# A four-layer attention kernel: layer 2's head-spread operand built in eight parts, and another table of steps for the stages without layer 2

## The chip, the cores and the metric

The kernel runs on one core of one Trainium2 chip. The metric is the device time of one execution in microseconds. Engines are named as in the profile: PE (TensorE), DVE (VectorE), ACT (ScalarE), POOL (GpSimd), SP (SyncE, which here only issues DMAs).

## What is computed

Four attention layers run one after the other on x (8 batches, 100 rows, 128 columns), 16 heads of 8. Layers 0, 1 and 3 attend to a context of 1444 keys; layer 2 attends to the context's first 100 rows with a causal mask, and has a feed-forward part.

```python
x = _L0_xattn_ref(x, ctx_1024, ...)    # rmsnorm(x), rmsnorm(ctx), attention, @ wo.T
x = _L1_xattn_ref(x, ctx_1024, ctx_1024, mask, ...)   # masked attention, @ Wo.T, + x, layer norm
x = _L2_xattn_ref(x, ctx_1024, ...)    # causal, so only the first 100 keys count; FF of 512, gelu
x = _L3_xattn_ref(x, ctx_1024, ctx_1024, ...)         # attention, + x, layer norm
# in each:
scores = einsum('bhqd,bhkd->bhqk', q, k) * scale
o = einsum('bhqk,bhkd->bhqd', softmax(scores), v)
```

## The kernel before

**Units, stages and steps.** The work on the long context is cut into 24 units: layer 0, 1 and 3 for each of the 8 batches. A unit's scores are made in 48 tiles, 12 chunks of about 120 keys by 4 groups of four heads (400 columns, `QW`). The whole program is a pipeline of stages n = -3 to 24, each of 48 steps j (`NSTEP`). In stage n the unit n is in its `exp` role (scores once more, exponential on ACT, product with the values into `acc`), unit n-1 is `post` (output, projection, norms), unit n+1 is `top` (values, maxima), and unit n+2 is `prep` (context, inputs, queries, keys); unit n+3 is `load`. Layer 2 has no unit of its own. Its attention (`att2`) is carried in stages 12 to 19 and its norm and feed-forward (`ff2`) in stages 13 to 20.

**What sets the order.** Every engine's order is written by hand from two tables: `AT` says at which step j of a stage the pieces of layers 0, 1 and 3 stand, `AT2` and `AT2_FF` do so for layer 2. In each step PE issues one score tile for the exponential (`sexp`, three banks), one score tile for the row maximum (`ring`), every fourth step 16 products into `acc`, and then whatever the tables put at that step. DVE takes the maximum tile into `mx` (L1251, in the first chunk L1249), then its share of the tables' pieces: `kp` (L1228 for layers 1 and 3, L1231 for layer 0) at the step after k0, k1 and k2, `qs` (L1238) at the step of q, output and norm pieces at steps counted from O (7) and wo (15), `ssq` (L1213) at 25 and 28. ACT takes the exponential at each step, and `kp`'s high part, the copies of xT, q and v at theirs. An engine works strictly in its written order, so that one that waits holds all that is behind it.

**The ring.** All of PE's products other than `sexp` and `acc` share four PSUM banks, `ring0` to `ring3`. `place` walks through all steps ahead of time and gives each use the bank that is free first by a table of holding times (`HOLD`); PE then waits, before it writes a bank, until the bank's last holder has been read (`await_read`). Keys hold their bank until DVE's `kp`, queries until DVE's `qs`.

**Layer 2's operand.** POOL turns layer 2's keys into an operand that is zero outside a head's 8 rows (`spread2`, L518): `kbd2` has two halves (high and low part, index i) of 16 heads by 100 columns. Its source is one half of `kq16`, the 16-bit copies of `k2`. PE's four score products of layer 2 (`scores2`, steps 20 to 23) wait for it. Behind `spread2` on POOL stands `root` (L506): `rstd`, the reciprocal root of the norm in `ff2`. DVE's `scale` (L1281) at step 13 waits for it. Behind `root` POOL spreads the next unit's queries into `qx` (L535) once DVE has made `qs`, and later takes the maxima off layer 2's scores (L526).

## Time and profile before

| what | value |
|---|---|
| median of 3 runs | 1046.35 us (1047.9, 1038.03, 1046.35) |
| the profiled execution | 1042.32 us; its span 1040.5 us |
| PE busy | 940.1 us, 90% |
| DVE busy | 852.9 us, 82% |
| ACT busy | 721.5 us, 69% |
| POOL busy | 376.2 us, 36% |
| mean granted TensorE clock | 0.967 of full speed |
| chain that ended last | PE 60%, DVE 26%, ACT 5%, issue 4%, POOL 3%, DMA 2% |

The profiled execution was 4.0 us below the median of the runs. Busy times are those of the records. PE's matmuls overlap: four products of 400 columns are issued in 0.17 us and the record of the group is 0.34 us long, so a gap between records of PE is about 0.17 us shorter than the gap between issues.

### The profile page before, as it was taken

What the parts mean: (1) busy time and instruction counts of PE and PEld (TensorE: products, weight loads), DVE (VectorE), ACT (ScalarE), POOL (GpSimd) and SP (SyncE); (2) the same over time, 40 slices, a digit from 0 to 9 for tenths busy, and PEclk for the clock granted to TensorE, in tenths of its full rate; (3) what the DMA queues carried; (4) which work ended last, traced back from release to release, by engine and by line L of the source; (5) the groups of instructions that cost most, each with busy time, mean ns of one, the idle gap of its engine ahead of it and who ended that gap; (6) DMA issues with size and microseconds to landing.
All of it is one profiled execution on the core that took longest, in us unless ns stands there. A gap on an engine that the chain in (4) does not pass through costs nothing.

```text
span 1040.5 us, 43899 instructions
## 1 busy us (share of the span) xinstructions
PE 940.1 (90%) x18826; PEld 554.9 (53%) x18826; DVE 852.9 (82%) x1804; ACT 721.5 (69%) x1637; POOL 376.2 (36%) x404
## 2 busy tenths in 40 slices
PE   1889999999989999999989899899989898999996
PEld 1345556555546555555555555555555555555552
DVE  7887899889778898888988787888797878779851
ACT  1129777777767777777767767677677666677776
POOL 3845445444323232322353444344352515122000
PEclk9669999999999999999999999999999898999999
DMA  8322313232222333233223131212121221222100
GB/s 227 111 63 65 93 50 89 70 78 60 79 84 61 97 99 96 60 95 96 62 85 86 37 88 52 73 35 72 37 70 49 61 56 53 56 66 62 53 4 6
DMA packets 63641, 73.75 MB, mean 71 GB/s; under 512 B 8130, under 2 KB 59114, under 8 KB 63318
## 3 DMA queue, kind: packets, MB, share of 16 engines
q1 hardware_dynamic: 63446, 70.92, 24.3%
q8 instruction: 150, 2.46, 1.0%
q14 instruction: 45, 0.37, 0.1%
HBM read 50.35 MB, written 18.15 MB: 66 GB/s over the span
## 4 chain that ended last, share of the span: by engine, by line
PE 60%; DVE 26%; ACT 5%; issue 4%; POOL 3%; DMA 2%; SPq 1%; POOLq 0%; ACTq 0%; DVEq 0%
PE ring L609 23%; PE sexp L609 13%; PE acc L779 13%; DVE mx L1251 7%; PE ring L652 5%; DVE mneg L1257 5%; DVE mx L1249 4%; POOL kbd L518 2%; PE ring L836 1%; PE ring L629 1%; ACT probs L1031 1%; DMA qx<-mrow 1%; DVE qs L1238 1%; PE ring L790 1%; DMA rows<-in_rows 1%
## 5 line engine op out<-in xcount | busy, mean ns | idle before, releaser
L1251 DVE TENSOR_TENSOR mx<-ring,mx 120x400 f16<-120x400 f32 (+1 forms) x1056 | 563.0, 564 | 111.2 <-PE ring L609 104.9
L1031 ACT ACTIVATE probs<-sexp 120x400 f32<-120x400 f32 (+1 forms) x1152 | 531.7, 508 | 174.4 <-PE sexp L609 171.9
L609 PE MATMUL ring<-qx,krep 96*32 96x400 f16 (+2 forms) x4608 | 415.0, 346 | 30.7 <-DVE mx L1249 13.3
L609 PE MATMUL sexp<-qx,krep 97*32 97x400 f16 (+2 forms) x4608 | 410.3, 339 | 11.4 <-ACT probs L1031 7.3
L779 PE MATMUL acc<-probs,vx 120*18 120x200 f32 (+1 forms) x4608 | 253.8, 337 | 0.8 <-ACT probs L1031 0.7
L609 PEld LDWEIGHTS ring<-qx,krep 96*32 96x32 f16 (+2 forms) x4608 | 129.7, 98 | 126.3 <-DVE mx L1251 36.2
L609 PEld LDWEIGHTS sexp<-qx,krep 97*32 97x32 f16 (+2 forms) x4608 | 131.5, 96 | 101.8 <-ACT probs L1031 34.6
L779 PEld LDWEIGHTS acc<-probs,vx 120*18 120x18 f32 (+1 forms) x4608 | 131.4, 99 | 66.9 <-issue 4.5
L498 POOL CAST ct<-ctf 128x480 f16<-128x480 f32 (+1 forms) x69 | 41.5, 601 | 202.7 <-PE ring L652 143.2
L535 POOL TENSOR_TENSOR qx<-qs,headmask 96x400 f16<-96x400 f16 x96 | 80.0, 862 | 73.8 <-DVE qs L1238 73.7
L500 POOL TENSOR_TENSOR ct<-ctf,ct 128x480 f16<-128x480 f32 (+1 forms) x69 | 76.4, 1107 | 5.5
L652 PEld LDWEIGHTS ring<-wv,ct 128*120 128x120 f16 (+1 forms) x864 | 54.8, 136 | 26.8 <-DVE mx L1251 11.9
L652 PE MATMUL ring<-wv,ct 128*120 128x128 f16 (+1 forms) x864 | 64.9, 226 | 2.5 <-DVE mx L1251 1.5
L1249 DVE CAST mx<-ring 121x400 f16<-121x400 f32 x96 | 52.7, 565 | 15.2 <-PE ring L609 15.1
L609 PE MATMUL ring<-ct,wk 128*32 128x480 f16 (+1 forms) x864 | 60.0, 383 | 4.1 <-DVE mx L1251 2.9
L506 POOL TENSOR_TENSOR rstd<-vare,half 100x1 f32<-100x1 f32 x24 | 13.3, 556 | 131.7 <-DVE vare L1273 131.7
L1257 DVE TENSOR_REDUCE mneg<-ring 100x8 f16<-100x968 f16 x48 | 55.3, 1154 | 1.0 <-PE ring L735 1.0
L1001 ACT COPY vx<-ring 120x512 f32<-120x512 f32 (+1 forms) x72 | 42.4, 589 | 13.2 <-PE ring L652 10.1
L991 ACT ACTIVATE kp<-ring,cols 128x480 f16<-128x480 f32 (+1 forms) x48 | 31.8, 663 | 26.2 <-PE ring L609 26.2
L518 POOL TENSOR_TENSOR kbd<-kq,heads 128x1600 f16<-128x1600 f16 x16 | 45.8, 2881 | 0.6
L513 POOL CAST kq<-k 128x200 f16<-128x200 f32 x8 | 2.8, 352 | 96.1 <-ACT v L1054 96.1
L545 POOL CAST maskb<-mask 100x480 bf16<-100x480 uint8 (+1 forms) x24 | 13.4, 597 | 62.4 <-DMA mask<-in_mask 62.4
(139 smaller groups left out, 895.6 us busy)
## 6 DMA issues: line engine op xcount, KB each, us to landing
krep<-kept SPq DMA_DIRECT2D x144, 120.0 KB, 2.8
ctf<-in_ctxT SPq DMA_DIRECT2D x16, 722.0 KB
kept<-kp SPq DMA_DIRECT2D x48, 240.0 KB, 3.1
krep<-kept SPq DMA_DIRECT2D x72, 121.0 KB, 2.6
kept<-kp SPq DMA_DIRECT2D x24, 242.0 KB, 2.8
nat<-in_ctx SPq DMA_DIRECT2D x8, 720.0 KB
maskexp<-maskmax SPq DMA_DIRECT2D x8, 281.2 KB, 3.4
anymask<-in_mask SPq DMA_DIRECT2D x1, 1128.1 KB, 10.0
```

Source lines behind the costliest of these rows:

```text
L498: pool.tensor_copy(ct[:, u.par, 0, c0:c0 + n], ctf[:, c0:c0 + n]).then_inc(sem["ct_high"], 1)
L500: pool.tensor_tensor(ct[:, u.par, 1, c0:c0 + n], ctf[:, c0:c0 + n], ct[:, u.par, 0, c0:c0 + n], ALU.subtract).then_inc(sem["ct_low"], 1)
L518: last = pool.tensor_tensor(kbd2[:, i, :, :], kq16[:, i, 0, :].unsqueeze(1).broadcast_to([128, H, S]), heads16[:, :].unsqueeze(2).broadcas ...
L535: last = pool.tensor_tensor(qx[0:PARTS, u.third, t, :, :], qs[:, t, :].unsqueeze(1).broadcast_to([PARTS, HT, S]), headmask16[:, :].unsquee ...
L609: last = run(out[g:g + m], w[:, g:g + m], x, **flags)
L652: last = pe.matmul(ps[0:r, D * i:D * i + D], ct[:, u.par, p, c0:c0 + r], wv16[:, w, u.L, :], start=(j == 0), stop=(j == 2))
L779: last = pe.matmul(acc[32 * q:32 * q + VW, 2 * S * side:2 * S * side + 2 * S], vx[0:r, u.par, PAIRS * c + 2 * t + p, :], probs[0:r, j % PR ...
L1001: act.copy(vx[0:r, u.par, a0:a1, :].rearrange("p a (f e) -> p a f e", f=2)[:, :, :, 0:DH], bank(f"v{g}", u)[0:r, 0:2 * DH * (a1 - a0)].rea ...
L1031: act.activation(probs[0:r, j % PR, :], sexp[j % SR][0:r, 0:QW], ACT.Exp).then_inc(sem["probs_ready"], 1)
L1249: op = dve.tensor_copy(dst, src)
L1251: op = dve.tensor_tensor(dst, src, dst, ALU.max)
L1257: dve.tensor_reduce(mneg[:, 8 * i:8 * i + 8], bank(f"mt{i}", u)[0:S, :].bitcast(F16).rearrange("s (h n) -> s h n", h=8)[:, :, 0:chunk(0)[1 ...
```

## The change

There are two edits. The first: POOL's two instructions of 1600 columns for `kbd2` become eight of 400, for each group t of four heads the high and the low half, and the semaphore `kbd2_ready` counts 4 per batch in place of 1. PE's `scores2` waits for part t+1 ahead of group t, where it waited once ahead of the first. The second: a new table `AT_PLAIN` holds in every stage in which neither `att2` nor `ff2` is there: stages -2 to 11 and 21 of those with a `prep` unit (stage 22 has values only). In it xT stands at step 18 (13 before), q at 20 (16), k1 at 22 (24), v0 at 24 (25), mk0 at 25 (26), v1 at 27 (28), mk1 at 28 (29), k2 at 30 (31), mk2 at 31 (32). k0 (10), OT (12), wo (15), v2 (33), the norm steps and the maxima stay. Since `place` gives out the banks from these steps, the banks of later products change as well.

```diff
+AT_PLAIN = dict(AT, xT=18, q=20, k1=22, v0=24, mk0=25, v1=27, mk1=28, k2=30, mk2=31)
...
-                          "kq2_high": 1, "kq2_low": 1, "kbd2_ready": 1, "s2_filled": 4, "s2_read": 4, "max2_ready": 4, "less2_ready": 4,
+                          "kq2_high": 1, "kq2_low": 1, "kbd2_ready": T, "s2_filled": 4, "s2_read": 4, "max2_ready": 4, "less2_ready": 4,
...
+        def steps_of(s):
+
+            return AT if s.att2 is not None or s.ff2 is not None else AT_PLAIN
...
-                for i in range(2):
-                    last = pool.tensor_tensor(kbd2[:, i, :, :], kq16[:, i, 0, :].unsqueeze(1).broadcast_to([128, H, S]),
-                                              heads16[:, :].unsqueeze(2).broadcast_to([128, H, S]), ALU.mult)
-                last.then_inc(sem["kbd2_ready"], 1)
+                for t in range(T):
+                    h = slice(HT * t, HT * t + HT)
+                    for i in range(2):
+                        last = pool.tensor_tensor(kbd2[:, i, h, :], kq16[:, i, 0, :].unsqueeze(1).broadcast_to([128, HT, S]),
+                                                  heads16[:, h].unsqueeze(2).broadcast_to([128, HT, S]), ALU.mult)
+                    last.then_inc(sem["kbd2_ready"], 1)
...
-                if t == 0:
-                    pe.wait_ge(*at("kbd2_ready", u, 1))
+                pe.wait_ge(*at("kbd2_ready", u, t + 1))
...
-                    if s.prep is not None and j == AT["q"]:
+                    if s.prep is not None and j == steps_of(s)["q"]:
                         queries(s.prep)
```

All other uses of `AT[...]` in the loops of PE, ACT and DVE and in `other_products` become `steps_of(s)[...]` in the same way.

**PE, steps 12 to 14 of stage 3.** `ident,oatt` is OT at step 12, `ident,xall` is xT, `qx,krep` into a ring bank is a maximum tile, into sexp the tile for the exponential. k0 was put into ring2 at step 10 before the change, and into ring3 after it. Before:

```order
L609 MATMUL ring3<-ident,oatt 32x100 x4
L609 MATMUL sexp1<-qx,krep 32x400 x3
L609 MATMUL sexp1<-qx,krep 25x400
L609 MATMUL ring0<-qx,krep 32x400 x4
L609 MATMUL ring2<-ident,xall 32x100 x4
L609 MATMUL sexp2<-qx,krep 32x400 x3
L609 MATMUL sexp2<-qx,krep 25x400
L609 MATMUL ring1<-qx,krep 32x400 x4
L779 MATMUL acc<-probs,vx 18x200 x8
```

Of the changed kernel, the same place:

```order
L617 MATMUL ring1<-ident,oatt 32x100 x4
L617 MATMUL sexp1<-qx,krep 32x400 x3
L617 MATMUL sexp1<-qx,krep 25x400
L617 MATMUL ring0<-qx,krep 32x400 x4
L617 MATMUL sexp2<-qx,krep 32x400 x3
L617 MATMUL sexp2<-qx,krep 25x400
L617 MATMUL ring3<-qx,krep 32x400 x4
L787 MATMUL acc<-probs,vx 18x200 x8
```

xT is gone from there, and the next to use k0's bank is the maximum tile of step 14, one `sexp` tile later.

**DVE, steps 15 to 24 of the same stage.** `y` (L1320) and `xall` (L1324) are the two pieces behind the projection, `qs` is the queries' piece, `kp` that of the keys. Before:

```order
L1251 TENSOR_TENSOR mx<-ring2,mx 120x400
L1320 TENSOR_TENSOR y<-ring0,rows 100x128
L1238 SCALAR_TENSOR_TENSOR qs<-qh,headmask,ring1 96x400
L1251 TENSOR_TENSOR mx<-ring3,mx 120x400
L1324 TENSOR_TENSOR xall<-y,xall 100x128
L1251 TENSOR_TENSOR mx<-ring0,mx 120x400
L1251 TENSOR_TENSOR mx<-ring2,mx 120x400
```

Of the changed kernel, from the same piece `y` on:

```order
L1327 TENSOR_TENSOR y<-ring1,rows 100x128
L1258 TENSOR_TENSOR mx<-ring3,mx 120x400
L1331 TENSOR_TENSOR xall<-y,xall 100x128
L1258 TENSOR_TENSOR mx<-ring2,mx 120x400
L1258 TENSOR_TENSOR mx<-ring0,mx 120x400
L1258 TENSOR_TENSOR mx<-ring3,mx 120x400
L1245 SCALAR_TENSOR_TENSOR qs<-qh,headmask,ring2 96x400
L1258 TENSOR_TENSOR mx<-ring1,mx 120x400
L1258 TENSOR_TENSOR mx<-ring0,mx 120x400
L1258 TENSOR_TENSOR mx<-ring1,mx 120x400
L1238 TENSOR_TENSOR kp<-ring3,kp 128x480
```

`qs` no longer stands between `y` and `xall` but three maximum tiles behind them, and three tiles ahead of the next keys' `kp`; before, nine stood between.

**POOL, in stage 13.** `rstd` is the root for layer 2's norm. Before:

```order
L513 CAST kq16<-k2 128x200
L515 TENSOR_TENSOR kq16<-k2,kq16 128x200
L518 TENSOR_TENSOR kbd2<-kq16,heads16 128x1600 x2
L506 TENSOR_TENSOR rstd<-vare,half 100x1
L545 CAST maskb<-mask8 100x484
```

Of the changed kernel:

```order
L519 CAST kq16<-k2 128x200
L521 TENSOR_TENSOR kq16<-k2,kq16 128x200
L526 TENSOR_TENSOR kbd2<-kq16,heads16 128x400 x8
L512 TENSOR_TENSOR rstd<-vare,half 100x1
L553 CAST maskb<-mask8 100x484
```

Nothing changes its place on POOL; `rstd` stands behind eight instructions in place of two.

## Rows read from the trace of the kernel before

**Rows 1.** Busy by stretch: us; PE, PEld, DVE, ACT, POOL (instructions); PEclk, DMA, GB/s

```profile
183.07:219.50 36.43, 35.58 (x733) 21.36 (x729) 32.14 (x65) 27.65 (x63) 16.80 (x16) 1.00 0.28 74
368.33:403.92 35.59, 34.34 (x736) 20.94 (x732) 30.46 (x61) 27.27 (x63) 9.94 (x13) 1.00 0.31 88
403.92:440.60 36.68, 34.70 (x736) 20.99 (x732) 32.60 (x69) 27.26 (x63) 10.54 (x14) 1.00 0.29 85
656.55:704.04 47.49, 43.56 (x915) 25.90 (x908) 39.47 (x92) 34.41 (x80) 19.58 (x20) 1.00 0.21 59
800.30:850.10 49.80, 44.59 (x888) 27.01 (x884) 40.80 (x90) 34.26 (x80) 19.72 (x20) 0.92 0.20 57
```

**Rows 2.** Timeline of PE, stage 3: start, us, line, out<-in, [idle before <-releaser]

```profile
197.26 0.38 PE L609 MATMUL ring<-ident,xall 100*32 100x100 f32 x8 [0.21 <-DVE kp L1231]
...
202.47 0.34 PE L609 MATMUL ring<-qx,krep 96*32 96x400 f16 x4
202.64 0.34 PE L609 MATMUL sexp<-qx,krep 97*32 97x400 f16 x4
203.26 0.35 PE L609 MATMUL ring<-qx,krep 96*32 96x400 f16 x4 [0.28 <-DVE mx L1251]
```

**Rows 3.** Timeline of PE, stage 9

```profile
416.38 0.38 PE L609 MATMUL ring<-ident,xall 100*32 100x100 f32 x8 [0.37 <-DVE kp L1228]
...
422.69 0.35 PE L609 MATMUL ring<-qx,krep 96*32 96x400 f16 x4 [0.28 <-DVE mx L1251]
...
425.32 0.79 PE L609 MATMUL ring<-ct,wk 128*32 128x480 f16 x12 [0.61 <-DVE mx L1251]
...
433.53 0.88 PE L652 MATMUL ring<-wv,ct 128*120 128x128 f16 x12 [0.25 <-DVE mx L1251]
```

**Rows 4.** Chain that ended last, stage 15: start, us, what

```profile
665.98 5.72 POOL kbd L518 x2
671.70 0.52 POOL rstd L506
```

**Rows 5.** Timelines of DVE and PE, stage 15

```profile
672.24 0.35 DVE L1281 SCALAR_TENSOR_TENSOR xn<-xn,rstd,rows 100x128 f32<-100x128 f32 x1 [1.19 <-POOL rstd L506]
```

```profile
677.42 0.70 PE L609 MATMUL ring<-kbd,kq 128*32 128x400 f16 x12
```

**Rows 6.** One line's instructions: ns min/median/max, first and last start, forms

```profile
L518 POOL TENSOR_TENSOR kbd<-kq,heads x16: 2857/2881/2906, 523.5 to 863.6; 128x1600 f16<-128x1600 f16 x16
```

```profile
L535 POOL TENSOR_TENSOR qx<-qs,headmask x96: 846/852/902, 29.3 to 961.7; 96x400 f16<-96x400 f16 x96
```

```profile
L1314 DVE TENSOR_TENSOR y<-y,xall x8: 278/292/2455, 765.5 to 1035.7; 100x128 f32<-100x128 f32 x8
```

**Rows 7.** Timeline of DVE, stage 18

```profile
811.47 0.98 DVE L1311 TENSOR_TENSOR y<-oatt,rows 100x128 f32<-100x128 f32 x1
...
812.85 2.46 DVE L1314 TENSOR_TENSOR y<-y,xall 100x128 f32<-100x128 f32 x1
...
817.21 0.34 DVE L1281 SCALAR_TENSOR_TENSOR xn<-xn,rstd,rows 100x128 f32<-100x128 f32 x1
```

**Rows 8.** Timeline of POOL, stages 17 and 18

```profile
762.09 5.72 POOL L518 TENSOR_TENSOR kbd<-kq,heads 128x1600 f16<-128x1600 f16 x2
...
776.87 0.85 POOL L526 TENSOR_TENSOR sc<-sc,max 100x400 f32<-100x400 f32 x1 [0.77 <-DVE max L1338]
```

```profile
809.44 5.72 POOL L518 TENSOR_TENSOR kbd<-kq,heads 128x1600 f16<-128x1600 f16 x2
...
826.51 0.85 POOL L526 TENSOR_TENSOR sc<-sc,max 100x400 f32<-100x400 f32 x1 [0.75 <-DVE max L1338]
```

**Rows 9.** Busy time by stretch, two microseconds each, stages 17 and 18

```profile
766.00:768.00 2.00, 0.28 (x11) 0.00 (x0) 2.00 (x2) 0.97 (x4) 2.00 (x2) 1.00 0.00 0
...
814.00:816.00 2.00, 0.00 (x2) 0.01 (x2) 2.00 (x3) 0.23 (x1) 1.72 (x2) 0.69 0.00 0
816.00:818.00 2.00, 2.00 (x28) 0.97 (x32) 2.00 (x7) 0.00 (x0) 0.00 (x0) 0.50 0.36 123
```

More of the change, by code:

```diff
@@ L271, in other_products @@
             for g in range(3):
-                if prep is not None and prep.L == 0 and j == AT[f"ct{g}"]:
+                if prep is not None and prep.L == 0 and j == steps_of(s)[f"ct{g}"]:
                     uses.append((f"ct{g}", prep))
-                if prep is not None and j == AT[f"k{g}"]:
+                if prep is not None and j == steps_of(s)[f"k{g}"]:
                     uses.append((f"k{g}", prep))
-                if prep is not None and prep.L == 1 and j == AT[f"mk{g}"]:
+                if prep is not None and prep.L == 1 and j == steps_of(s)[f"mk{g}"]:
                     uses.append((f"mk{g}", prep))
-                if top is not None and j == AT[f"v{g}"]:
+                if top is not None and j == steps_of(s)[f"v{g}"]:
                     uses.append((f"v{g}", top))
@@ L281, in other_products @@
                            ("mn", top)):
-                if u is not None and j == AT[use] and not (use in ("OT", "wo") and u.L == 3):
+                if u is not None and j == steps_of(s)[use] and not (use in ("OT", "wo") and u.L == 3):
                     uses.append((use, u))
@@ L1086, in stage @@
                     for g in range(3):
[L1087 removed]
+                        if s.prep is not None and s.prep.L == 0 and j == steps_of(s)[f"ct{g}"]:
                             context(s.prep, g, s.top)
[L1089 removed]
+                        if s.prep is not None and j == steps_of(s)[f"k{g}"]:
                             keys(s.prep, g)
[L1091 removed]
+                        if s.prep is not None and s.prep.L == 1 and j == steps_of(s)[f"mk{g}"]:
                             mask(s.prep, g)
[L1093 removed]
+                        if s.top is not None and j == steps_of(s)[f"v{g}"]:
                             vals(s.top, g)
[L1095 removed]
+                    if s.post is not None and s.post.L < 3 and j == steps_of(s)["OT"]:
                         output_back(s.post)
[L1097 removed]
+                    if s.prep is not None and j == steps_of(s)["xT"]:
                         inputs(s.prep)
[L1099 removed]
+                    if s.prep is not None and j == steps_of(s)["q"]:
                         queries(s.prep)
@@ L1106, in stage @@
                                        ).then_inc(sem["mask_counted"], 1)
-                    if s.top is not None and j == AT["mn"]:
+                    if s.top is not None and j == steps_of(s)["mn"]:
                         maximum_rows(s.top)
@@ L1416, in stage @@
                         for part in range(4):
-                            if j == AT["O"] + 1 + part:
+                            if j == steps_of(s)["O"] + 1 + part:
                                 output(u, part)
-                            if u.L == 3 and j == AT["O"] + 5 + part:
+                            if u.L == 3 and j == steps_of(s)["O"] + 5 + part:
                                 centre(u, y[:, 0, :], "own_o", part)
-                            if u.L == 1 and j == AT["wo"] + 3 + part:
+                            if u.L == 1 and j == steps_of(s)["wo"] + 3 + part:
                                 centre(u, y[:, 0, :], "own_y", part)
                         for part in range(2):
-                            if u.L < 3 and j == AT["wo"] + 1 + part:
+                            if u.L < 3 and j == steps_of(s)["wo"] + 1 + part:
                                 projected(u, part)
-                            if u.L == 1 and j == AT["scale"] + part:
+                            if u.L == 1 and j == steps_of(s)["scale"] + part:
                                 scale(u, residual(u), "x_next", part)
-                            if u.L == 3 and j == AT["scale"] + part:
+                            if u.L == 3 and j == steps_of(s)["scale"] + part:
                                 if part == 1:
@@ L1432, in stage @@
                     for g in range(3):
-                        if s.prep is not None and j == AT[f"k{g}"] + 1:
+                        if s.prep is not None and j == steps_of(s)[f"k{g}"] + 1:
                             keys(s.prep, g)
-                    if s.prep is not None and j == AT["q"]:
+                    if s.prep is not None and j == steps_of(s)["q"]:
                         queries(s.prep)
                     for part in range(2):
-                        if s.load is not None and s.load.L == 0 and j == AT["power"] + 3 * part:
+                        if s.load is not None and s.load.L == 0 and j == steps_of(s)["power"] + 3 * part:
                             power(s.load, part)
                     for i in range(2):
-                        if s.top is not None and j == AT[f"mt{i}"]:
+                        if s.top is not None and j == steps_of(s)[f"mt{i}"]:
                             maxima(s.top, i)
```

33 lines of the change are left out of this document (13 added, 20 removed).

## The prediction

> **What bounds the kernel now.** I read the busy times by stretch first. Between two copies of the maxima, that is over one stage, a stage without layer 2 takes 36.43 us (stage 3, layer 0 in preparation), 35.59 (stage 8) and 36.68 (stage 9, where a layer 1 unit is normed as well); one with layer 2 takes 47.49 (stage 15) and 49.80 (stage 18) [rows 1]. PE is busy for 35.58 of 36.43 us and 43.56 of 47.49, DVE for 32.14 and 39.47. PE sets the pace, and what can be gained is where PE waits for a bank of the ring that DVE has not read.
>
> Second, the timeline of PE. In it four products are issued 0.17 us apart from the next four though each record is 0.34 long, so an idle time shown is short of the real stall by 0.17 [rows 2]. Stage 3 then has two stalls that this change touches. xT waits for k0's bank, 0.21 + 0.17 = 0.38 us, and a maximum tile some steps behind the queries waits 0.28 + 0.17 = 0.45 [rows 2]. Stage 9 has four: 0.37 + 0.17 = 0.54 at xT, 0.45 behind the queries, 0.61 + 0.17 = 0.78 at k1, and 0.25 + 0.17 = 0.42 at v2, which stands two steps behind k2 [rows 3].
>
> Third, the chain that ended last, in the stages with layer 2. In stage 15 it runs through both `kbd` instructions (5.72 us), then `rstd` (0.52) [rows 4], then DVE's `xn`, which had waited 1.19 us for it [rows 5]. PE's first product on `kbd` starts at 677.42 [rows 5], and `kbd` was whole at 665.98 + 5.72 = 671.70 [rows 4]: nobody waits for the operand itself. What is late is the small root that stands behind it on POOL. The two microsecond slices and DVE's rows of stages 17 and 18 I come to below.
>
> **Edit 1, eight parts for two, stages 13 to 16.** An instruction of 1600 columns takes 2.881 us, one of 400 columns of the same kind takes 0.852 [rows 6]. The slope is (2.881 - 0.852) / 1200 = 1.69 ns a column, the fixed part 0.852 - 400 x 0.00169 = 0.18 us. Eight parts take 8 x 0.852 = 6.82 us where two took 5.72 [rows 4]: +1.1 us. The bounds are 8 x 2.857 / 4 = 5.71 (no fixed part, +0) and 8 x 0.902 = 7.22 (+1.5) [rows 6]. I take 6.82, since `qx` is the same operation with the same kinds of operands. `rstd` and the waiting `xn` move by as much, and the chain passes through them. So the early first part brings nothing here, and the late end costs 4 x 1.1 = +4.4 us. Stage 12 has no `ff2`, so no root behind `kbd`: 0. The three added waits of PE are met long before, 0.
>
> **Edit 1, stages 17 to 19.** Here DVE's `y` (L1314), two operands in SBUF, takes 2.455 us at most and 0.292 as a median [rows 6]. In stage 18 it runs from 812.85 to 815.31, and `kbd` from 809.44 to 815.16; the one ahead, L1311, runs from 811.47 to 812.45, and the first `kbd` ended at 809.44 + 2.86 = 812.30 [rows 7, 8]. Both end just behind an end of a POOL instruction. I read it as DVE being held until the POOL instruction that is under way is over. With parts of 0.85 us it is held for 0.85 at most, on the mean 0.43: L1314 takes about 0.7, 1.7 us less. But `xn` stands behind it and needs `rstd`, at 809.44 + 6.82 + 0.52 = 816.78, and started at 817.21 [rows 7, 8]. So of the 1.7 us only 817.21 - 816.8 = 0.4 arrive: 3 x 0.4 = -1.2 us.
>
> DVE gets its turn at the end of a POOL instruction, and hardly holds POOL back: the two `kbd` of stage 18, with L1311 falling between them, took the same 5.72 us as those of stage 15 [rows 4, 8]. So I put nothing on POOL for it. The Trainium skill (SBUF — State Buffer, section "SBUF: two separate sides") says that the port pair which VectorE and GpSimd share is a lock, held for a whole instruction, and that the loser blocks fully, whichever it is. By the first half of that rule L1314's wait shrinks as I have it; by the second each such VectorE operation between two parts adds its own length to POOL, and the sum would be that of the last rival below.
>
> **Edit 1 and the clock.** In stage 18 the stall behind L1314 leaves PE idle, and the granted clock falls from 1.00 to 0.50 (1.2 GHz of 2.4) at 814 to 816; in stage 17 PE is busy 0.28 us of two and the clock stays at 1.00 [rows 9]. The price is the time from `kbd` to the first subtraction of a maximum: 826.51 - 809.44 = 17.07 us with the fall, 776.87 - 762.09 = 14.78 without [rows 8]. That is 2.3 us. In stage 19 the clock falls at the same place. If DVE's stall is cut into pieces, as above, PE takes several tiles in between; I take it that both falls go: -4.6 us. Bounds: 0 and -4.6.
>
> **Edit 2.** Behind k0 the next user of its bank comes one `sexp` tile (0.17 us) later and no longer is xT, so that 0.38 becomes about 0.2 and 0.54 about 0.35; moved to 18, xT finds a bank read long ago. I take 0.2 us per stage. The queries, now at 20, lie clear of `y` and `xall`, and nothing of DVE's other than one norm step is at their side, so I take the 0.45 as gone. k2 a step earlier puts its `kp` two steps ahead of v2: the 0.42 goes. Of the 0.78 at k1 in stages with a norm I take half, 0.4: the norm steps stand where they did, and DVE's load in that stretch is the same. What hides the rest: `qx` is spread on POOL in four parts of 0.852 [rows 6] and is needed at step 35; even four steps later (four times 36.43 / 48 = 3.0 us) it is ready by about step 28.
>
> Sums: stages 0 to 5, (0.2 + 0.45) x 6 = 3.9. Stages 6 to 8, (0.2 + 0.45 + 0.42) x 3 = 3.2. Stages 9 to 11, (0.2 + 0.45 + 0.42 + 0.4) x 3 = 4.4. Stages -2, -1, 21: 0, the first two wait for loads and for DVE. Together -11.5. The bounds are 0 and all of the stalls, 0.83 x 6 + 1.25 x 3 + 2.19 x 3 = 15.3.
>
> **Sum.** +4.4 - 1.2 - 4.6 - 11.5 = -12.9 us. Against the profiled execution: 1042.3 - 12.9 = 1029.4. The median of the runs shown lies 4.0 above that execution, so the median would be 1033; I write 1032, a little under, since a collision of `xall` and of two norm steps with `qx` on POOL goes too, which I can't size.
>
> **Rivals.**
> - *The stalls move instead of going.* DVE's work in the stretch from step 16 to 34 is the same and it is busy 32.14 of 36.43 us [rows 1]; q, k1 and v0 now stand at 20, 22 and 24, close together. For it: PE's slack over DVE is small. Against: a stall moves only where DVE is behind by three tiles. Then edit 2 gives a third, 4 us, and the sum is -5.4: 1037 by the profile, 1040 by the median.
> - *The clock falls elsewhere.* In stages 13 to 16 the wait for `rstd` grows from 1.19 to 2.3 us, nearly the length at which stage 18 fell. Four falls cost 4 x 2.3 = 9.2, and the sum is -3.7, near 1042. For it: rows 9 show that the same idle time may or may not bring a fall. Against: PE has tiles in hand during a part of the wait.
> - *Slower: two banks held at once.* q at 20 and k1 at 22 each take a bank until ACT and then DVE have gone over them, as k0 does, where it costs 0.54 [rows 3]. If the maxima have two banks left for four steps, and each of these steps stalls by that much, that is 4 x 0.54 = 2.2 us a stage, over 12 stages 26, and the sum is +13: 1059 by the median. It turns the sum to a loss from a new stall of 12.9 / 12 = 1.1 us a stage. Against: DVE comes to these pieces with less behind it than it does now.
> - *POOL is held by DVE between parts.* Eight parts have seven places between them where two had one. If in stages 13 to 19 three two-operand pieces of DVE get in, each 0.29 long [rows 6], and POOL waits them out, `rstd` is late by 7 x 3 x 0.29 = 6 us more in all; the sum is -6.8, near 1039. Against: the unchanged 5.72 above. It is what the page's rule gives.
>
> **How the numbers follow.** Chances: forecast 0.46 (by its own bounds 1025 to 1037); stalls move 0.22; clock falls elsewhere 0.14; POOL held 0.07; slower 0.11. A measurement of this kernel tells about 1% from no change, that is 10.5 us. Of the forecast nine tenths lie over 1% faster, of the second a third (less lost than I say), of the others little: 0.41 + 0.07 + 0.03 = 0.51 faster. Slower by over 1% is the two banks' case and a little of the clock's: 0.12. The rest, 0.37, is within 1%. The range goes from 1022 (all the stalls of edit 2 gone, 3.8 more, and some of the collisions) to 1047, which leaves the slower case and part of the clock's out.
>
> **What would show it.** In the profile of the changed kernel: eight `kbd` of about 0.85 us, 6.8 in all, with `rstd` right behind; DVE's `xn` in stages 13 to 16 waiting 2.2 to 2.4 us; L1314's longest under 1.2 us; no clock of 0.50 inside stages 18 and 19; stage 3 at 35.8, stage 8 at 34.5 and stage 9 at 35.2 us; stage 15 at 48.6. I am wrong if stages 3 and 9 are as long as before, if a stall of over 0.4 us stands at k1 or v0 of every stage, if PE waits for `kbd` in `scores2`, or if the granted clock falls in stages 13 to 16.

## The result and the profile after

The changed kernel takes 1034.64 us in the median (1031.91 to 1039.88, 20 runs), the kernel before 1044.57 in the same comparison (1038.03 to 1049.48, 20 runs). The ratio is 0.9911, with a 95% interval of 0.9897 to 0.9925: 0.9% faster. That is within the 1% that I had called the limit of what can be told from no change; the interval does exclude 1. I had written 1032 us, with a range of 1022 to 1047, and "faster by over 1%" as the likeliest case.

The page of the changed kernel, its head, its rows of slices and its chain:

```profile
span 1030.1 us, 43971 instructions
...
PE 934.3 (91%) x18826; PEld 559.9 (54%) x18826; DVE 837.4 (81%) x1804; ACT 717.6 (70%) x1637; POOL 382.4 (37%) x452
...
PEclk9669999999999999999999999999999999999999
...
PE 60%; DVE 22%; POOL 6%; ACT 5%; issue 4%; DMA 2%; SPq 1%; POOLq 0%; ACTq 0%; DVEq 0%
```

The span is 10.4 us shorter (1040.5 before). PE still has the longest busy time and the largest part of the chain, so what moved are stalls and the granted clock.

The stretches of stages 3, 8, 9, 15 and 18, cut at the same copies of the maxima and in the same columns as [rows 1]:

```profile
182.85:219.24 36.39, 35.78 (x733) 21.82 (x729) 31.70 (x65) 27.29 (x62) 16.76 (x16) 1.00 0.27 74
368.18:403.32 35.14, 34.37 (x736) 21.20 (x732) 29.94 (x61) 26.94 (x62) 9.89 (x13) 1.00 0.31 89
403.32:438.65 35.33, 34.54 (x736) 21.57 (x732) 31.57 (x69) 26.93 (x62) 10.40 (x14) 1.00 0.31 88
653.98:702.24 48.26, 43.33 (x915) 25.94 (x908) 39.19 (x92) 34.42 (x81) 20.45 (x26) 1.00 0.20 58
797.16:843.96 46.80, 42.54 (x900) 25.47 (x892) 38.92 (x91) 34.05 (x80) 20.63 (x26) 1.00 0.22 61
```

Stage 3 is as long as it was, stages 8 and 9 are shorter by 0.45 and 1.35 us, stage 15 is longer by 0.77 and stage 18 shorter by 3.00. The profiled executions are not all typical of their kernels: the changed kernel's took 1031.91 us (2.7 under its median), that of the parts alone 1039.63 (0.6 under), and that of the table alone 1034.4, the fastest of its 12 (5.5 under). The whole table, as differences of stage lengths to the kernel before in one profiled execution of each (us; "parts only" and "table only" are the first two experiments below, "root ahead" is the fifth):

| stages | forecast | after | parts only | table only | root ahead, eight parts |
|---|---|---|---|---|---|
| 2, 3, 4, 5 | -0.65 each | -0.33, -0.04, +0.03, -0.49 | +0.02, -0.01, +0.01, -0.18 | -0.32, -0.12, +0.07, -0.82 | 0.00, +0.07, +0.20, -0.79 |
| 7, 8 | -1.07 each | -0.54, -0.45 | 0.00, +0.01 | -0.53, -0.43 | -0.53, -0.43 |
| 9, 10, 11 | -1.47 each | -1.35, -1.65, -1.77 | +0.01, -0.13, +0.04 | -1.51, -1.51, -1.80 | -1.54, -1.64, -1.54 |
| 13, 14, 15, 16 | +1.1 each | +1.54, +1.54, +0.77, +0.52 | +0.87, +1.31, +0.63, +2.67 | +0.01, -0.01, -0.25, -0.35 | -1.82, -0.87, -1.06, +0.11 |
| 17 | -0.4 | -1.81 | -1.81 | -1.28 | -0.86 |
| 18, 19 | -2.7 each | -3.01, -3.28 | -1.78, -3.95 | +0.02, 0.00 | -2.06, -5.17 |
| 20 | 0 | -1.46 | -0.40 | +0.11 | -1.46 |
| 21 | 0 | +0.44 | 0.00 | +0.46 | +0.44 |

Stages 0, 1 and 6 moved by -0.43, +0.88 and +1.11, where -0.65, -0.65 and -1.07 were forecast; stage -1 took -0.34, stage 12 -0.28. Stage 6 lies between -1.4 and +1.9 over the experiments, and much of that is the clock: it is shortest with the table alone, whose clock stays at 1.00 there, where that of the kernel before has a mean of 0.96. All of it adds up to -10.4 us.

The eight parts. One line's instructions (ns: minimum, median, maximum), then the timelines of POOL and DVE in stage 16:

```profile
L526 POOL TENSOR_TENSOR kbd<-kq,heads x64: 847/855/904, 518.1 to 858.9; 128x400 f16<-128x400 f16 x64
```

```profile
711.42 6.59 POOL L526 TENSOR_TENSOR kbd<-kq,heads 128x400 f16<-128x400 f16 x8
717.97 0.55 POOL L512 TENSOR_TENSOR rstd<-vare,half 100x1 f32<-100x1 f32 x1
...
718.55 0.35 DVE L1288 SCALAR_TENSOR_TENSOR xn<-xn,rstd,rows 100x128 f32<-100x128 f32 x1 [2.43 <-POOL rstd L512]
```

A part takes 0.855 us, eight of them 6.59 where two took 5.72 [rows 4]; the root stands right behind, and DVE waits 2.43 us for it, where it waited 1.19 [rows 5].

DVE and then POOL in stage 18, the place of [rows 7, 8]:

```profile
808.37 0.61 DVE L1318 TENSOR_TENSOR y<-oatt,rows 100x128 f32<-100x128 f32 x1
...
809.38 0.45 DVE L1321 TENSOR_TENSOR y<-y,xall 100x128 f32<-100x128 f32 x1
...
813.58 0.35 DVE L1288 SCALAR_TENSOR_TENSOR xn<-xn,rstd,rows 100x128 f32<-100x128 f32 x1 [1.26 <-POOL rstd L512]
```

```profile
806.35 6.68 POOL L526 TENSOR_TENSOR kbd<-kq,heads 128x400 f16<-128x400 f16 x8
...
820.57 0.85 POOL L534 TENSOR_TENSOR sc<-sc,max 100x400 f32<-100x400 f32 x1 [0.75 <-DVE max L1345]
```

`y` (L1314 before, L1321 now) takes 0.45 us where it took 2.46, the other `y` 0.61 for 0.98, and from `kbd` to the first subtraction of a maximum it is 820.57 - 806.35 = 14.22 us, for 17.07.

The clock, in two-microsecond stretches. First the kernel before at the border of stages 16 and 17 and in stage 19, then the changed kernel at the same two places:

```profile
750.00:752.00 2.00, 2.00 (x33) 1.25 (x28) 0.92 (x3) 1.15 (x4) 0.00 (x0) 0.50 0.04 8
...
868.00:870.00 2.00, 2.00 (x32) 0.93 (x24) 1.88 (x8) 0.36 (x1) 0.00 (x0) 0.50 0.39 132
```

```profile
749.00:751.00 2.00, 2.00 (x45) 1.36 (x37) 1.30 (x3) 1.40 (x4) 0.00 (x0) 1.00 0.00 0
...
864.00:866.00 2.00, 2.00 (x42) 1.63 (x38) 0.72 (x2) 0.95 (x2) 2.00 (x4) 0.51 0.00 0
```

To compare kernels I cut stages 11 to 21 into stretches of one microsecond and added up the length of each times what its clock lacked to 1.00, where that was over 0.03. By stage, in us:

| kernel | 13 | 14 | 15 | 16 | 17 | 18 | 19 | 20 | sum |
|---|---|---|---|---|---|---|---|---|---|
| before | 0 | 0 | 0 | 0.85 | 0.85 | 4.00 | 5.18 | 1.06 | 11.9 |
| after | 1.71 | 1.71 | 0 | 0 | 0 | 0 | 1.71 | 0 | 5.1 |
| parts only | 0 | 0 | 0.43 | 2.96 | 0 | 1.71 | 1.11 | 0.60 | 6.8 |
| table only | 0 | 0 | 0 | 0 | 0 | 3.88 | 5.19 | 1.17 | 10.2 |
| root ahead, eight parts | 0 | 0 | 0.42 | 1.64 | 1.69 | 1.34 | 0 | 0 | 5.1 |

About 6.8 us of clock were won in this execution. One execution is one draw, though. Span and mean granted clock are known of every execution. Span times what its mean clock lacked to 1.00 is the same sum over the whole span, start included. It is the most that the clock can have cost, since PE also waits in it. What is left of the span is in the last column (us):

| kernel | executions | clock lost, mean | the rest, mean |
|---|---|---|---|
| before (beside the two halves) | 23 | 32.6 | 1010.0 |
| after | 20 | 27.4 | 1006.0 |
| parts only | 12 | 25.4 | 1012.4 |
| table only | 12 | 34.5 | 1003.2 |

The standard errors are 0.8 to 1.6 us in the third column and 0.9 to 1.2 in the fourth. So the change wins 5.2 us of clock and 4.0 of the rest. The parts win 7.2 us of clock and lengthen the rest by 2.4. The table shortens the rest by 6.8 and wins no clock (+1.9, about its error); the execution that its stage lengths are from lost 20.7 us, 14 less than its mean.

### The profile page after: what moved, and what is told of

The parts are those of the page before. It is cut to its first block, busy times and chain, and to the rows that moved or that the text cites. A ratio compares the mean times of both kernels' runs of the same rounds, so it can differ in the third digit from the quotient of the medians.

```text
span 1030.1 us, 43971 instructions
## 1 busy us (share of the span) xinstructions
PE 934.3 (91%) x18826; PEld 559.9 (54%) x18826; DVE 837.4 (81%) x1804; ACT 717.6 (70%) x1637; POOL 382.4 (37%) x452
## 4 chain that ended last, share of the span: by engine, by line
PE 60%; DVE 22%; POOL 6%; ACT 5%; issue 4%; DMA 2%; SPq 1%; POOLq 0%; ACTq 0%; DVEq 0%
PE ring L617 23%; PE sexp L617 14%; PE acc L787 13%; DVE mx L1258 6%; PE ring L660 5%; DVE mneg L1264 5%; POOL kbd L526 5%; DVE mx L1256 4%; ACT probs L1038 2%; PE ring L843 1%; PE ring L637 1%; DMA rows<-in_rows 1%; DVE kp L1235 1%; DVE ssq L1220 1%; PE ring L798 1%
## 5 line engine op out<-in xcount | busy, mean ns | idle before, releaser
L617 PE MATMUL ring<-ct,wk 128*32 128x480 f16 (+1 forms) x864 | 63.5, 383 | 1.8 <-DVE mx L1258 0.8
L526 POOL TENSOR_TENSOR kbd<-kq,heads 128x400 f16<-128x400 f16 x64 | 53.0, 863 | 0.6
```

The costliest lines, as they stand in the source:

```text
L526: last = pool.tensor_tensor(kbd2[:, i, h, :], kq16[:, i, 0, :].unsqueeze(1).broadcast_to([128, HT, S]), heads16[:, h].unsqueeze(2).broadca ...
L617: last = run(out[g:g + m], w[:, g:g + m], x, **flags)
```

## The experiments

All were compared with the kernel before on their own chip. The theory at the start was that of the prediction: the late root costs stages 13 to 16, the shorter holds of DVE pay in 17 to 19, the new table pays in the stages without layer 2.

### The two halves apart

The parts alone:

```diff
-AT_PLAIN = dict(AT, xT=18, q=20, k1=22, v0=24, mk0=25, v1=27, mk1=28, k2=30, mk2=31)
+AT_PLAIN = AT
```

> Edit 1 alone: eight parts, the old steps in all stages. Theory (the eight parts lengthen kbd and so rstd in stages 13 to 16, and take DVE's hold of 2.4 us away in 17 to 19): stages -1 to 11 and 21 as before within 0.1 us each; stages 13 to 16 longer by 0.5 to 1.5 us each; 17 to 19 shorter by 1.8 to 3.3; in all 5 to 6 us less than before, ratio near 0.995. Rival (the gain of the change lies in the new table alone): no less than before, ratio 1.000 or above.

Measured: 1040.19 us against 1044.91, ratio 0.9956 (0.9936 to 0.9976).

The table alone (`kbd` in two instructions again):

```diff
-                for t in range(T):
-                    h = slice(HT * t, HT * t + HT)
-                    for i in range(2):
-                        last = pool.tensor_tensor(kbd2[:, i, h, :], ...)
-                    last.then_inc(sem["kbd2_ready"], 1)
+                for i in range(2):
+                    last = pool.tensor_tensor(kbd2[:, i, :, :], ...)
+                last.then_inc(sem["kbd2_ready"], T)
```

> Edit 2 alone: two parts of 1600 columns, the new steps. Theory (the edits act in different stages and add up): stages 9 to 11 shorter by 1.3 to 1.8 us each, 7 and 8 by 0.5, 2 to 5 by 0.2 on the mean; stages 13 to 19 as before; ratio near 0.995. Rival (the two edits need each other, because the ring's banks are given out anew everywhere): stages 13 to 19 differ from before by over 0.5 us each.

Measured: 1039.92 us, ratio 0.9958 (0.9937 to 0.9978).

The halves add up: 0.9956 x 0.9958 = 0.9914 beside 0.9911. So each gives 0.4%, some 4.5 us, and the theory's two totals (0.995 for each) came. By the table of stages the parts leave stages 2 to 11 alone, and the table alone leaves stages 13 to 16, 18 and 19. Stage 17 is the exception, the only one over the 0.5 us of the second rival: it is 1.28 us shorter with the table alone too. The clock goes with it: the kernel before had the half clock at the border of stages 16 and 17, the table alone had it not (0 in both stages), with the same instructions there. In the two microseconds ahead of that spot PE is busy for 1.05 us in both kernels, and the clock fell in one and not in the other. If that is what stage 17 won with the table alone, 1.3 of its 1.81 us are the clock, and 0.5 is left for the parts.

### The root ahead of the operand

In stages 13 to 16 the eight parts cost time because the root stands behind them. It waits for DVE's `vare`, which lies near `kbd`'s start. So the root goes ahead of `kbd`, first with nothing that waits for its end, once with eight parts and once with two.

```diff
                 pool.tensor_tensor(kq16[:, 1, :, :], k2[:, :, :], kq16[:, 0, :, :], ALU.subtract).then_inc(sem["kq2_low"], 1)
+                if ff2 is not None:
+                    root(ff2)
                 pool.wait_ge(*at("kq2_low", u, 1))
                 for t in range(T):
```

> The changed kernel with layer 2's root put ahead of the eight parts on POOL (behind the two casts). Theory (the parts cost time only because the root stands behind them): DVE's wait for rstd of 2.3 to 2.4 us in stages 13 to 16 and 1.25 in 17 to 19 is gone; stages 13 to 16 go below those of before, by 1 us each, so 2 us each less than in the changed kernel; 17 to 19 less by another 1; in all 10 us less than the changed kernel, ratio to before near 0.982. Rival (DVE's own work is the bound there and the wait only fills a gap): less than 2 us in all.

Measured: 1066.95 us against 1044.91, ratio 1.0221 (1.0193 to 1.025).

> As the run before, but with two parts of 1600 columns again. Theory (a part holds DVE until it is over, so short parts help whoever's root comes first): L1314 of DVE is again 2.4 us in stages 17 to 19 and the oatt piece about 0.9 in 13 to 16; stages 17 to 19 are longer than with eight parts by 1.5 us each, 13 to 16 by 0 to 0.4. Rival (with the root early the length of the parts does not matter): within 0.3 us a stage of the run before, everywhere.

Measured: 1059.69 us, ratio 1.0147 (1.0118 to 1.0177).

Both are slower than the kernel before, and neither theory nor rival of the two had that. POOL, DVE and PE of the one with eight parts, in stage 14, and a stretch of two microseconds:

```profile
619.27 0.55 POOL L512 TENSOR_TENSOR rstd<-vare,half 100x1 f32<-100x1 f32 x1 [0.20 <-DVE vare L1282]
619.78 6.53 POOL L528 TENSOR_TENSOR kbd<-kq,heads 128x400 f16<-128x400 f16 x8
...
621.28 5.18 DVE L1317 TENSOR_TENSOR oatt<-oatt,rows 100x128 f32<-100x128 f32 x1
...
626.51 0.56 PE L619 MATMUL ring<-ident,oatt 100*32 100x100 f32 x8 [4.48 <-DVE oatt L1317]
```

```profile
626.00:628.00 2.00, 1.49 (x24) 0.76 (x28) 2.00 (x5) 0.73 (x2) 0.31 (x1) 0.50 0.00 0
```

DVE's `oatt`, two operands in SBUF and 0.28 us long when nothing holds it, takes 5.18 us and ends at 626.46, just behind the end of all eight parts at 626.31. Some six ends of a part went by without its getting a turn. PE then waits 4.48 us and comes back at half clock; over its six executions this kernel loses 50.6 us of clock, for 32.6 before. In stage 12 of the same kernel, which has no root, the same piece beside the same eight parts took 0.45 us. With two parts it is held 4.26 to 4.46 us, past the end of the first.

What differs from the changed kernel at this spot is what POOL has waited for. There the wait on `kq2_low` right ahead of the first part is for the end of the instruction that stands just before it. Here that wait still stands ahead of the first part, but the root has come between: the semaphore was there long before, nothing waits for the root's own end, and `kbd` starts at 619.78, before the root's record ends (619.27 + 0.55 = 619.82). So the next kernels put a wait for the root's own completion behind it:

```diff
                 if ff2 is not None:
                     root(ff2)
+                    pool.wait_ge(*at("rstd2_ready", ff2, 1))
                 pool.wait_ge(*at("kq2_low", u, 1))
                 for t in range(T):
```

> Layer 2's root ahead of the eight parts, as in the slow run before, and POOL waits for the root's own completion before it starts the parts. Theory (behind the root, which covers 100 partitions and is not waited for, POOL's instructions overlap so that DVE finds no gap between them and is held until the last part is over; a wait lets them start together again): DVE's oatt piece takes 0.4 to 0.7 us in place of 5.2, DVE does not wait for rstd, stages 13 to 16 at 46 to 47 us, 17 to 19 at 46, ratio to before 0.980 to 0.985. Rival (DVE is held by where its piece falls in the parts, 1.5 us behind their start, and not by what stands ahead of them): the piece again over 5 us and a ratio near 1.02.

Measured: 1027.85 us against 1043.9, ratio 0.9835 (0.98 to 0.9869). The same places as above:

```profile
613.57 0.55 POOL L512 TENSOR_TENSOR rstd<-vare,half 100x1 f32<-100x1 f32 x1 [0.19 <-DVE vare L1283]
614.20 6.71 POOL L529 TENSOR_TENSOR kbd<-kq,heads 128x400 f16<-128x400 f16 x8
...
615.63 0.38 DVE L1318 TENSOR_TENSOR oatt<-oatt,rows 100x128 f32<-100x128 f32 x1
...
618.18 0.34 DVE L1291 SCALAR_TENSOR_TENSOR xn<-xn,rstd,rows 100x128 f32<-100x128 f32 x1
```

One added wait, which costs POOL some 0.1 us a stage (`kbd` starts 614.20 - 613.57 = 0.63 us behind the root's start, for 0.51 without it), turns 1066.95 into 1027.85. `oatt` is back at 0.38 us, and `xn` no longer waits for the root. `oatt` starts 615.63 - 614.20 = 1.43 us behind the first part's start, for 621.28 - 619.78 = 1.50 in the slow kernel, so the rival, that its place in the parts holds it, fell; the time is as the theory had it.

The same with two parts, and with four of 800 columns:

> The same with two parts of 1600 columns. Theory: the hold of DVE ends with the first part, oatt about 0.8 us in 13 to 16, L1314's successor 2.4 us in 17 to 19, so these three stages 1 to 3 us longer each than with eight parts; 13 to 16 within 0.5 us. Rival (the length of a part does not matter once the root is early): within 0.3 us of the run with eight parts in all stages.

Measured: 1045.53 us, ratio 1.0011 (0.9986 to 1.0036). The second `y` takes 2.45 us, as expected, and the rival fell. But `oatt` takes 1.57 to 1.75 us and not 0.8, since it starts 1.3 to 1.4 us behind the first part's start and not 2.0; in stages 13 to 16 this kernel is longer than the one with eight parts by 3.21, 1.92, 1.81 and -0.41 us, not within 0.5. The clock is in that: it lost 1.71 and 1.23 us in stages 13 and 14, where with eight parts it lost none, and none in stage 16, where with eight parts it lost 1.64. The rest was not traced.

> As e5, but four parts of 800 columns. Theory (fixed part of 0.18 us an instruction, slope 1.69 ns a column, DVE held until the part under way is over): the four parts take 4 x 1.53 = 6.1 us in all against 6.6, the held pieces of DVE 0.3 to 1.3 us against 0.45 to 0.6 with eight parts and 1.7 to 2.45 with two; stages 13 to 16 as with eight within 0.4, 17 to 19 between the runs with eight and with two. Rival (only the total length of kbd matters): stages 17 to 19 shorter than with eight parts.

Measured: 1028.21 us, ratio 0.9845 (0.9818 to 0.9872). POOL and DVE of two parts in stage 17, then of four parts in stage 18:

```profile
761.81 5.72 POOL L527 TENSOR_TENSOR kbd<-kq,heads 128x1600 f16<-128x1600 f16 x2
...
763.07 1.74 DVE L1319 TENSOR_TENSOR y<-oatt,rows 100x128 f32<-100x128 f32 x1
...
765.23 2.45 DVE L1322 TENSOR_TENSOR y<-y,xall 100x128 f32<-100x128 f32 x1
```

```profile
801.87 6.05 POOL L529 TENSOR_TENSOR kbd<-kq,heads 128x800 f16<-128x800 f16 x4
...
804.10 0.97 DVE L1324 TENSOR_TENSOR y<-y,xall 100x128 f32<-100x128 f32 x1
```

With two parts the first `y` ends at 764.81, and the first part at 761.81 + 2.86 = 764.67; the second `y` ends at 767.68, and the second part at 767.53. Once POOL has waited for the end of the instruction just ahead of the parts, DVE is held until the next end of a part and no longer: these pieces take 2.46 us at most with 1600 columns, 0.98 with 800, 0.61 with 400 (0.55 in the kernel with the root ahead). Others take up to 1.30 with 800 and 0.94 with 400 (`xn`, 0.34 when nothing holds it), their own length included, so the hold itself is still less than a part of 1.52 or 0.86. Four parts cost POOL 6.05 us, eight 6.71, and the two kernels run equally fast; stages 17 to 19 lie between those of eight and two parts (0.26, 0.44 and 2.13 us longer than with eight), as the theory of four parts had it, and its rival fell. Stages 13 to 16 differ from those with eight by 0.56, 0.31, -0.15 and -1.42 us, so two of the four are outside the 0.4 expected.

With the table of steps the same in all four, the two questions part cleanly:

| | root behind `kbd` | root ahead, with a wait |
|---|---|---|
| two parts | 0.9958 | 1.0011 |
| eight parts | 0.9911 | 0.9835 |

An early root pays only with short parts, since it brings DVE's pieces into `kbd`; short parts pay more with the root ahead of them.

### The table of steps, apart

xT and q alone, and the keys and values alone:

```diff
-AT_PLAIN = dict(AT, xT=18, q=20, k1=22, v0=24, mk0=25, v1=27, mk1=28, k2=30, mk2=31)
+AT_PLAIN = dict(AT, xT=18, q=20)
```

> The changed kernel, but of the new steps only xT (18) and q (20); k1, k2, v0, v1 and the masks at their old steps. Theory (in stages 2 to 5 the moved k2, closer behind DVE's second ssq, gives back at v2 what xT and q bring): stages 2 to 5 shorter than before by 0.5 us or more each, where the whole table gave 0 to 0.3; stages 7 and 8 about as with the whole table, 9 to 11 shorter than before by 1 or more. Rival (the 0.45 behind the queries is only shifted by q's own move): stages 2 to 5 as before within 0.1 us.

Measured: 1031.13 us, ratio 0.9879 (0.9838 to 0.992).

```diff
+AT_PLAIN = dict(AT, k1=22, v0=24, mk0=25, v1=27, mk1=28, k2=30, mk2=31)
```

> The changed kernel, but of the new steps only k1, k2, v0, v1 and the masks; xT and q at their old steps. Theory: stages 2 to 5 longer than before by 0.2 to 0.6 us each (the stall at v2 without the gain at the queries); 9 to 11 less than half of the 1.5 us that the whole table gave. Rival (the keys' move is what helps): stages 9 to 11 shorter than before by over 1 us each.

Measured: 1044.63 us, ratio 1.0 (0.9978 to 1.0022).

Both keep the eight parts. The new steps of keys and values do harm: without them stage 3 is 0.63 us shorter than in the changed kernel and stages 8 and 9 are 0.30 and 0.51; with them alone stages 3 and 8 are 0.57 and 0.36 longer than before. For stages 2 to 4 the reason can be read at the end of stage 3 of the changed kernel. PE, then DVE:

```profile
210.81 0.34 PE L617 MATMUL sexp<-qx,krep 97*32 97x400 f16 x4
211.21 0.35 PE L617 MATMUL ring<-qx,krep 96*32 96x400 f16 x4
211.39 0.34 PE L617 MATMUL sexp<-qx,krep 97*32 97x400 f16 x4
211.70 0.35 PE L617 MATMUL ring<-qx,krep 96*32 96x400 f16 x4
212.18 0.88 PE L660 MATMUL ring<-wv,ct 128*120 128x128 f16 x12
```

```profile
209.20 1.21 DVE L1220 TENSOR_REDUCE ssq<-sq 120x8 f32<-120x1024 f32 x1
...
212.04 0.64 DVE L1238 TENSOR_TENSOR kp<-ring,kp 128x480 f16<-128x480 f32 x1
```

And PE in the kernel before, where v2 does not wait:

```profile
212.15 0.35 PE L609 MATMUL ring<-qx,krep 96*32 96x400 f16 x4
212.43 0.88 PE L652 MATMUL ring<-wv,ct 128*120 128x128 f16 x12
```

From one issue to the next it is 0.40 us where 0.17 is due, then 0.31 where 0.17 is due, and 0.48 at v2, where 0.28 is due: stalls of 0.23, 0.14 and 0.20 us that stage 3 did not have. k2 now stands at step 30, two steps behind `ssq` (step 28, 1.21 us of DVE), which has put DVE behind; its `kp` comes at 212.04, and v2 waits for a bank. (`ssq` stands in the stages up to 4 alone; stages 7 to 11 come below.) Of the 0.38 and 0.45 [rows 2], 0.22 stayed behind k0, and 0.57 came here: 0.79 for 0.83, and the stage is 0.04 us shorter. With the keys and values alone both old stalls stand there unchanged (PE, stage 3 of that kernel):

```profile
197.62 0.38 PE L617 MATMUL ring<-ident,xall 100*32 100x100 f32 x8 [0.21 <-DVE kp L1238]
...
203.61 0.35 PE L617 MATMUL ring<-qx,krep 96*32 96x400 f16 x4 [0.27 <-DVE mx L1258]
```

So the whole gain of the table comes from xT and q, and k and v give part of it back. Both theories held in the main and both rivals fell: with xT and q alone stages 2 to 5 are 0.32 to 0.71 us shorter, with k and v alone 0.24 to 0.58 longer, and stages 9 to 11 of the latter are no shorter than before (+0.19, +0.05, +0.16).

### What the experiments point to

The root ahead with its wait, eight parts, and only xT and q moved:

> Both findings together: layer 2's root first with a wait behind it, eight parts, and of the new steps only xT and q. Theory (the gains lie in different stages and add up): stages 2 to 5 shorter than before by 0.5, 7 and 8 by 0.75, 9 to 11 by 1.9, 13 to 15 by 1, 17 to 19 by 2 to 5; ratio to before near 0.980, 3 us below the run with the root first and the whole table. Rival (a gain in one place is given back in the next stage): no better than 0.9835.

Measured: 1023.23 us against 1044.51, ratio 0.9791 (0.9761 to 0.9822). The total is as expected, and the gains do add up. By stages only 17 missed (0.83 us shorter for 2 to 5), and 14 and 15 a little (1.02 and 0.75).

The same with v2 a step later in the stages without layer 2 (`AT_PLAIN = dict(AT, xT=18, q=20, v2=34)`):

> As the run before, and v2 at step 34 in place of 33 in the stages without layer 2. Theory (the 0.42 us that is left at v2 in stages 6 to 11 is a bank that DVE frees late because of the keys' piece of step 32): the stall goes, stages 7 to 11 shorter by 0.3 to 0.4 each. Rival (DVE is late by its whole load there): the stall only moves one step, under 0.1 us a stage.

Measured: 1021.66 us, ratio 0.9771 (0.9737 to 0.9804), the lowest of all, though not apart from the one ahead by more than the intervals. v2's stall in stage 9 is gone. In the kernel ahead (the row below) v2 is issued 0.60 us behind the tile before it, where 0.28 is due, a stall of 0.32; now 0.25 appears before a tile. Stages 7 to 11 are shorter by 0.09, 0.09, 0.09, 0.21 and 0.60. In 7 to 9 this stall moved, as the rival had it, for 10 less so; what went in 11 was not traced.

```profile
430.76 0.88 PE L663 MATMUL ring<-wv,ct 128*120 128x128 f16 x12 [0.25 <-DVE mx L1261]
```

And xT a step later, at 14, in the stages with layer 2 (`AT_FULL = dict(AT, xT=14)`):

> As e9, and xT at step 14 in place of 13 in the stages with layer 2. Theory (xT's wait of 0.55 us for the bank of k0 is PE's own, as in the other stages): the stall shrinks to 0.2 and stages 13 to 16 are shorter by 0.2 to 0.3 us each. Rival (in these stages DVE sets the pace and a stall of PE costs nothing): no change over 0.1 us a stage.

Measured: 1024.96 us, ratio 0.9804 (0.9773 to 0.9834). The stall of 0.54 us at xT goes, with 0.24 ahead of a tile in its place, as expected, and stages 13 to 16 move by -0.01, -0.12, -0.73 and +0.92 us: no gain can be told, and the theory's 0.2 to 0.3 a stage isn't seen.

## Why the prediction came out as it did

The total was near (-12.9 forecast, -10.4 in the profiled spans, -9.9 between the medians), but not for the reasons of the sum. Apart, I had -1.4 us for the parts and -11.5 for the table; the runs gave -4.6 (0.44%) and -4.4 (0.42%). Two errors of opposite sign. Cut the other way, by the means over all executions, the parts without their clock came to +2.4 for +3.2 forecast, their clock to -7.2 for -4.6, and the table without clock to -6.8 for -11.5. The terms of the parts were sound, that of the table was 1.7 times too large, and that the total came near is in good part luck. The 4.0 us that I added for the median came from three runs; over 20 the profiled execution lies 2.3 under the median of the kernel before, so from there the sum gives 1031.7. And of the signs of being wrong that I had named two came: stage 3 is as long as before, and the granted clock falls in stages 13 and 14. Stage 3 took 36.39 us for 35.8 forecast, stage 8 35.14 for 34.5, stage 9 35.33 for 35.2, stage 15 48.26 for 48.6.

**Eight parts: right.** 0.855 us each (0.852 forecast), nobody waits for the operand, 6.59 us in all for 6.82. A step from one part to the next is (6.59 - 0.855) / 7 = 0.82, a little less than a record, so the term is +0.9 for +1.1. `xn` waits 2.43 us, as forecast (2.2 to 2.4). In stages 13 to 15 of the parts alone, where the clock hardly fell, the cost was 0.87, 1.31 and 0.63.

**Clock falls elsewhere: the rival came half true.** The wait of stages 13 and 14 brought the half clock. PE and two microseconds of stage 13:

```profile
572.10 0.35 PE L617 MATMUL ring<-which,bq 36*32 36x400 f16 x3 [2.20 <-DVE mx L1258]
```

```profile
574.00:576.00 2.00, 2.00 (x36) 1.64 (x32) 1.49 (x3) 1.62 (x4) 0.72 (x1) 0.55 0.00 0
```

In stages 15 and 16 a stall of the same kind (idle 1.90 us in stage 16, for 2.20 here) brought none. Each of these falls costs 1.71 us of clock (3.4 us at 1.2 GHz of 2.4), where I had 2.3. The four stages came to +4.4, my number, out of smaller delays and two falls that it didn't hold: luck again.

**The hold of DVE in stages 17 to 19: right.** `y` went from 2.46 to 0.45 us, and only about 0.5 us a stage arrived, since `xn` waits for the root (1.26 us): 0.4 was forecast. Stage 17's other 1.3 us I put down to the clock at its start, which I had not looked at: my rows of the clock [rows 9] were two places, and the kernel before has the half clock also at the borders of stages 16/17, 18/19 and 19/20.

**The clock in stages 18 and 19: right in kind, wrong in one place, too small in size.** Stage 18 has none left. In stage 19 it falls still, at about 862.5, for 1.71 us instead of the 5.18 of that stage before; I had said that none would be inside. The rows give no reason why 19 and not 18, for PE's stalls are the same in both: 

```profile
814.46 0.35 PE L617 MATMUL ring<-qx,krep 96*32 96x400 f16 x4 [0.96 <-DVE mx L1258]
815.45 0.38 PE L617 MATMUL ring<-ident,att 100*32 100x100 f32 x8 [0.64 <-DVE mx L1258]
```

(stage 18; in stage 19 they are at 861.26 and 862.25, with the same two numbers). One stall of 2.58 us has become 1.13 and 0.81 (0.96 and 0.64, and 0.17 each). I reckoned 4.6 us of clock for stages 18 and 19; with the borders and stages 13 and 14 it came to 6.8 net in this execution. Stage 20's -1.46 is of this kind for 1.06.

**POOL held by DVE: the rival fell.** `kbd` takes 6.59 us in stage 16, where one two-operand piece of DVE gets in (`oatt`), and 6.68 in stage 18, where three do (both `y` and `xn`). A `y` is 0.29 long by itself, so POOL did not wait out even one. The rule (the Trainium skill, SBUF — State Buffer, section "SBUF: two separate sides") has both sides block; the first half agrees with this case where POOL has waited (`y` took 2.46 us beside parts of 2.88 and 0.45 beside parts of 0.855), the second is not seen in these rows. In the experiment with the root ahead and no wait for it DVE was held through several instructions, which the rule doesn't say.

**xT and q: right on the mean.** With only these moved, stages 2 to 5 came to -0.32, -0.67, -0.46 and -0.71 and stages 7 and 8 to -0.74 and -0.75, for 0.65 forecast. The 0.45 behind the queries went, and 0.22 stayed behind k0, as I had it.

**k2 a step earlier: wrong, the largest miss.** The step was "k2 a step earlier puts its `kp` two steps ahead of v2: the 0.42 goes". It did not. A product of v is issued 0.28 us behind a tile even when nothing holds it, so the 0.42 was 0.31 to begin with; in the changed kernel's stage 9, v2 stalls for 0.35, now behind `kp`, and the tile ahead of it for 0.25. PE, then DVE:

```profile
431.59 0.88 PE L660 MATMUL ring<-wv,ct 128*120 128x128 f16 x12 [0.28 <-DVE kp L1235]
```

```profile
430.33 0.57 DVE L1258 TENSOR_TENSOR mx<-ring,mx 120x400 f16<-120x400 f32 x1 [0.87 <-PE ring L617]
430.83 0.71 DVE L1235 SCALAR_TENSOR_TENSOR kp<-ring,cols,kp 128x480 f16<-128x480 f32 x1
```

I counted steps on PE and not what DVE does between them. In stages 2 to 4 that is `ssq` at 28, which makes it late. In stages 7 to 11 there is no `ssq`, and DVE isn't late: in stage 9 it had been idle for 0.87 us just before the maximum tile ahead of `kp`. `kp` ends at 430.83 + 0.71 = 431.54, and only then does v2 start. I read it as v2 waiting for the keys' own bank, held longer than the steps between k2 and v2 last. Against xT and q alone that took back 0, 0.63, 0.49 and 0.22 us in stages 2 to 5 and 0.20 and 0.30 in 7 and 8, and is the first rival, "the stalls move", in this half of the table. Only in stages 9 to 11 the sum held (-4.8 for -4.4), by two errors that cancel: the stall at v2 stayed, and the 0.78 at k1 went altogether and not by half. That one goes with xT and q alone as well, where k1 stands at its old step. In those stages, too, leaving k and v at their old steps gave 0.2 to 0.5 us more.

**Stage 21: not foreseen.** It is 0.44 us longer. I put it at 0, as a stage without much on it. The kernel with xT and q alone has +0.42 there, that with k and v alone +0.06, so it comes from xT or q; by which wait was not traced.

**Two banks held at once: the slower case fell.** No stage stalls behind q and k1 by anything near 0.54 four times; no stage without layer 2 is over 0.9 us longer other than stage 6, whose +1.11 is inside its own scatter over the experiments.

## What to carry to other kernels

Moving a step on the bottleneck engine off one stall wants a look at the engine that frees the buffers: what long piece stands just ahead of the moved step's partner there, and how long the buffer is held even when that engine isn't late. A small instruction that others wait for goes ahead of the long ones, and a long POOL instruction is cut where VectorE has two-operand work beside it; neither alone gave what both did. And if VectorE is held far longer than one POOL instruction, see whether POOL had waited for the end of the instruction just ahead of the run; an older wait that is met by then did not help here. Last, granted clock can be as large an item as the stalls: compare it over all executions before reading stages of one.
